# A column of zeros, written by GpSimd behind every single gather of the three edge passes

## The reference

```python
x = _layernorm(x + _L0_gnn_ref(x, edge_index, ...))            # max over edges of relu([x_i, x_j - x_i] @ W1 + b1) @ W2 + b2
x = _layernorm(x + _L1_gnn_ref(x, edge_index, edge_attr, ...)) # mean of edge_attr by src, then a two-layer network
x = _layernorm(x + _L2_gnn_ref(x, src, dst, ...))              # mean over edges of x[src], gates, linear
x = _layernorm(x + _L3_gnn_ref(x, ntype, etype, src, dst, ...))# attention of 4 heads over edges, typed weights
```

## Time and profile before

| | us |
|---|---|
| time, median of 2 runs | 19,879.55 (19,871.68 to 19,887.42) |
| the profiled execution: span from first to last instruction | 21,982.3 |
| busy in it: POOL, DVE, PE, PEld, ACT | 15,097.0, 6911.8, 4774.0, 4149.9, 1772.2 |
| gathers, 3 x 3125, busy in b, c, d | 3014.6, 3299.2, 3021.6 |
| scatter-adds, 3125, busy | 4984.9 |

### The profile page before, as it was taken

The page is one execution under the profiler, slowest core; times in us unless marked ns, Lnnn a source line. Parts: engine busy times, 40 slices in busy tenths (PEclk is TensorE's granted clock), DMA queues, the critical chain, the costliest instruction groups (busy, mean ns, idle before and its releaser), DMA issues. The chain is left out here.

```text
span 21982.3 us, 148548 instructions
## 1 busy us (share of the span) xinstructions
PE 4774.0 (22%) x30182; PEld 4149.9 (19%) x30182; DVE 6911.8 (31%) x16401; ACT 1772.2 (8%) x6281; POOL 15097.0 (69%) x13304
## 2 busy tenths in 40 slices
PE   4444444444423333333320000000041000000002
PEld 4444444444412222222210000000031000000001
DVE  3333333333312222222241111111122444444444
ACT  1111111111100000000010000000021000000001
POOL 5888888888876666666657777777724666666664
PEclk8555555555555555555555555555576555555555
DMA  4444444444422222222231111111122222222222
GB/s 93 53 52 52 52 52 53 50 53 52 52 48 65 65 65 65 63 65 64 65 59 48 47 47 46 47 47 46 43 68 89 87 89 89 87 90 87 89 89 38
DMA packets 1456154, 1380.95 MB, mean 63 GB/s; under 512 B 777810, under 2 KB 1260924, under 8 KB 1455996
## 3 DMA queue, kind: packets, MB, share of 16 engines
q0 software_dynamic: 775408, 541.25, 17.1%
q1 hardware_dynamic: 662716, 736.98, 10.3%
q10 hardware_dynamic: 18000, 102.41, 1.1%
HBM read 762.18 MB, written 617.56 MB: 63 GB/s over the span
## 5 line engine op out<-in xcount | busy, mean ns | idle before, releaser
L500 POOL DMA_INDIRECT agg<-sums,ag_idx x3125 | 4984.9, 1595 | 1166.4 <-issue 1118.5
L534 POOL DMA_INDIRECT gat<-tab_t,gi x3125 | 3021.6, 967 | 1752.5 <-issue 928.0
L534 POOL DMA_INDIRECT gat<-tab_b,gi x3125 | 3014.6, 965 | 1752.6 <-issue 931.3
L534 POOL DMA_INDIRECT gat<-tab_x,gi x3125 | 3299.2, 1056 | 1100.9 <-issue 1061.1
L842 PE MATMUL bank<-at,same 128*128 128x64 f32 x6250 | 1882.7, 431 | 3281.7 <-issue 1057.3
L842 PEld LDWEIGHTS bank<-at,same 128*128 128x128 f32 x6250 | 1570.5, 311 | 3419.7 <-issue 1813.5
L908 PE MATMUL pair<-ident,tails 128*64 128x128 f32 (+1 forms) x20 | 4.9, 419 | 9304.2 <-DVE tails L1209 4931.4
L908 PEld LDWEIGHTS pair<-ident,tails 128*64 128x64 f32 (+1 forms) x20 | 3.0, 167 | 9305.2 <-DVE tails L1209 4931.6
L1302 DVE TENSOR_TENSOR run_sb<-p,gat 128x320 f32<-128x320 f32 x625 | 317.1, 507 | 3710.6 <-DMA gat<-tab_x,gi 3710.6
L1164 DVE TENSOR_TENSOR run_sb<-p,bank 128x320 f32<-128x320 f32 x625 | 304.9, 488 | 3177.7 <-remote 2346.6
L876 PE MATMUL bank<-ident,ub 128*128 128x128 f32 x1250 | 413.0, 434 | 3494.1 <-DVE ub L1192 2228.1
(11 more groups left out here) (263 smaller groups left out, 13806.5 us busy)
## 6 DMA issues: line engine op xcount, KB each, us to landing
edge<-start_rows SPq DMA_DIRECT2D x250, 800.0 KB
run<-run_sb SPq DMA_DIRECT2D x250, 800.0 KB
run<-run_sb SPq DMA_DIRECT2D x125, 900.0 KB
start_rows<-zeros ACTq DMA_DIRECT2D x125, 800.0 KB, 3.5
at<-in_edge_attr SPq DMA_DIRECT2D x125, 800.0 KB
tab_t<-trow SPq DMA_DIRECT2D x98, 512.0 KB, 2.6
agg<-sums,ag_idx POOLq DMA_INDIRECT x3125
gat<-tab_b,gi POOLq DMA_INDIRECT x3125
```

The costliest lines, as they stand in the source:

```text
L500: pool.indirect_dma_start(agg_d[r], rows(agg_d[r], ag_idx[:, k, r:r + 1]), sums[:, k, r, :], None, bounds_check=AGR - 1, oob_is_err=True, ...
L534: pool.indirect_dma_start(gat[:, k, s, 0:width], None, table, rows(table, gi[tp][:, s, k:k + 1])).then_inc(g_in[c][k], 16)
```

## The change

In each of the three passes a function `breathe` is called behind every gather. It waits until the memset behind the gather before has completed (`p_beat` has reached the number of memsets so far), has a no-op that carries this wait, and lets GpSimd write zeros into a new column `beat` of 128 x 1 numbers; this counts `p_beat` up by one. The first memset of all has no wait. `done` carries the count over from pass to pass. Nothing reads `beat`.

```diff
--- before.py
+++ after.py
@@ -127,6 +127,7 @@
         iota_bf = sb("iota_bf", [P, P], BF16)
         spare_i = sb("spare_i", [P, 1], I32)
         spare = sb("spare", [P, 1])
+        beat = sb("beat", [P, 1])
         marks = sb("marks", [P, 20])
         eps_c = sb("eps_c", [P, 1])
         far_c = sb("far_c", [P, 1])
@@ -285,6 +286,7 @@
         ch_pre, ch_k = sem("ch_pre"), sem("ch_k")
         ch_n = {c: sem(f"ch_n{c}") for c in "123"}
         o_out = sem("out_written")
+        p_beat = sem("pool_beat")
 
         def run_view(tp, width):
             return run_sb[tp][:, :, 0:KS * width].rearrange("p s (k f) -> p s k f", f=width)
@@ -522,6 +524,13 @@
             for i in range(2):
                 pool.wait_ge(l_out[i], 16 + 8 * NBAT)
 
+            def breathe(c, n, opening):
+                done = "bcd".index(c) * NG * SUB
+                if done or not opening:
+                    pool.wait_ge(p_beat, n + done)
+                    pool.nop(nofuse=True)
+                pool.memset(beat[:], 0.0).then_inc(p_beat, 1)
+
             def gathers(c, table, width, staged, per, used):
                 def body(t, tp, first):
                     pool.wait_ge(staged, (t + 1) * per)
@@ -533,6 +542,7 @@
                         for s in range(SUB):
                             pool.indirect_dma_start(gat[:, k, s, 0:width], None, table,
                                                     rows(table, gi[tp][:, s, k:k + 1])).then_inc(g_in[c][k], 16)
+                            breathe(c, t * COLS + (k * SUB + s), first and k + s == 0)
                 each_iteration(pool, body)
 
             def node_rows(c, run_d, car, width, n):
```

## The result

| | before | changed | ratio |
|---|---|---|---|
| median, us (2 runs each) | 19,879.55 | 20,049.8 (20,048.06 to 20,051.54) | 1.0086 [1.0069, 1.0103] |
| profiled execution: span, us | 21,982.3 | 20,046.3 | |

The change costs 170 us, 0.9%, where 1169 us were forecast. The profiled execution of the changed kernel is no longer than its runs, so profiling by itself does not lengthen this kernel. There is no trace of the kernel before at 19,880 us. Every ratio of an experiment is against the kernel before on its own chip.

What follows compares the result with a forecast made beforehand. GpSimd's gathers, 1.25 us each, were taken to bound the three edge passes. Memset 844, wait 46 and fetches 279 us sum to 1169 us on 19,879.55, giving 21,049 us (chance 0.53), range 19,850 to 22,280 us.

Steps and rivals of the forecast that it cites:

- The bound: Three edge passes: GpSimd's row of gathers, 1.25 us each, sets the time; what is added to the pitch adds 9375 times.
- The premise on the 2103 us: Profiled execution is 2103 us longer than the median; runs without a profile were taken to have hardly any of the stalls.
- The memset, 844 us: Behind each gather on GpSimd: one memset adds 0.09 us, 9375 times, 844 us; bounds 0.03 and 0.12 us each.
- Rival 4: Between gathers: the 0.30 us gap vanishes behind a memset, 0.20 us gained per gather, -1875 us, 18,005 us; chance 0.08.
- The estimate from its cycles, 390 us: Memset part priced by the skill page: 50 cycles at 1.2 GHz, 0.042 us a memset, 390 us in place of 844.
- The wait, 46 us: GpSimd's sequencer: new wait hidden behind the current gather, except 0.25 us at 186 back edges: 46 us, bounds 0 and 75.
- The fetches, 279 us: Loop bodies grow, so an instruction fetch pause shows 1.5 us per round trip, 186 times: 279 us, bounds 0 and 446.
- Rival 1: Edge passes: a memset costs 0.03 us and fetches nothing, 281 us, 20,161 us; chance 0.17.
- Rival 2: Stalls of b and d exist without a profile and absorb the memsets; only pass c pays, 374 us, 20,254 us; chance 0.10.
- Rival 3: Each memset is paid like a gather with its own gap, 0.40 us, 3750 us in all, 23,630 us; chance 0.12.
- a distance of under 1.29 us: Sign that the forecast is wrong: two gathers' starts under 1.29 us apart in the changed profile, where 1.34 was expected.

Runs made afterwards that it cites:

- f2: Changed kernel with two one-column memsets behind each gather, the second one counting: 21,606.66 us, 0.9826 of the kernel before.
- e3: Changed kernel with a memset of 128x128 instead of 128x1: 21,776.28 us, 0.9853 of the kernel before.
- e4: Changed kernel with a memset of 128x512 instead of 128x1: 23,956.89 us, 1.0902 of the kernel before.
- f1: Changed kernel with a 128x512 memset, each waiting for the memset two back, so one more gather is queued: 23,801.37 us, 1.0823 of the kernel before.
- e5: Changed kernel with two more sequencer no-ops behind each memset: 21,818.82 us, 0.9873 of the kernel before.
- e6_waits_only: Changed kernel without memset: register operation, always fulfilled wait and two no-ops behind each gather, the second counting: 21,550.56 us, 0.98 of the kernel before.

## Why the prediction was wrong

**The bound** was right: the passes go at GpSimd's pitch, 1.25 us, and what lengthens the distance between gathers lengthens the time. The premise on the 2103 us was half right. The first runs seem indeed to have hardly any of the stalls: take the changed kernel's time outside its three passes, 20,046 - 12,054 = 7992 us, off the 19,880 us, and 11,888 us are left for the passes, by this estimate 170 us over the bare pitch. The reason given, that the stalls come of profiling, was wrong: the changed kernel's profiled execution has hardly any (12 us), and on other chips the runs of the kernel before take 22,000 us too.

**The memset, 844 us: this is the step that failed.** The prediction put it as "Bounds: 0.03 and 0.12 us; below, nothing, if it fits into the 0.30 us between two gathers. I take 0.09 us, because a one-column instruction behind a long one of another kind is the nearest case". The end that it named and didn't take is what happened: the cost is 0, for one and for two memsets (f2), whose gathers start 1.249 us apart like those before. The rows of the start give what a memset costs in a queue of memsets, but the pitch of the gathers is not the sum of what is queued. It has 0.30 us in which the engine can do something else, of which 0.16 remained behind the memset in e3, e4 and f2. The mistake was to let these two alternatives, a free slot and a serial price, share one term: a cost of zero should have been a rival with a chance of its own. Rival 4 had the other half of it: the gap is used, but doesn't vanish behind a memset.

The Trainium skill, "GPSIMD Engine Reference", section 2.1, says that the completion of one instruction doesn't hold back the next; the two memsets 0.03 us apart in f2 agree. The estimate from its cycles, 390 us, added to the time what runs in a gap: measured was 0.

**The wait, 46 us.** The run-ahead of one gather is enough in the usual stretch, as predicted: the median distance did not change. At the back edges no distance stands out either, their median is 1.249 us in pass b as well; 0 us, the lower bound.

**The fetches, 279 us.** Right in kind and wrong in cause: a pause that the longer queue hides comes bare when one gather is queued, f1 against e4 shows it. The price of one was nearly right: 2.3 us, less 0.6 covered, is 1.68 us, where the prediction had 2.4 less 0.9, 1.5 us. But it comes 99 times, every 95 gathers, and not 186 times, once per round trip: 167 us. That this is near 279 us is partly luck, since the pauses of the loops are not those of the earlier trace rows: they come without instruction packets, and e5 excludes the number of instructions.

The Trainium skill, "Runtime: NRT & Kernel Launch", section Instruction fetch mechanics, has the crossing of a block mostly hidden. In the gather loops here the regular pauses hang neither on the number of instructions nor on packets of the instruction queues, so nothing in these runs contradicts it.

**The rivals.** Rival 1 came nearest in time (20,161 us), with a mechanism that isn't this one: the cost was in pauses and not in memsets. Rival 2, that the stalls of b and d stay and cover the change, did not hold in the changed kernel's first profile, which has none; where such stalls are, on the other chips, the change even gains. Rival 3 is refuted by the pitch.

**What would show it**: the text named the test that it then failed, a distance of under 1.29 us, and the trace has 1.25.

**A better version** than before on these chips is e6_waits_only, with 2% less; it has no memset. Whether it gains, costs or does nothing where the kernel before takes 19,880 us was not measured, since no experiment ran on such a chip.

## What to carry to other kernels

Where a queue of equal DMA instructions has a constant gap in front of each, price a small instruction between them both ways, in the gap and in series, and give each its chance. The wait that shortened the queue cost nothing at the median here; it cost at the rare long pauses that the queue used to hide. So look for them in the sequencer's records, compare the same places in both traces, and find by another count what they are tied to. Whether they are fetches, the packets of the instruction queues say. And compare the span of the profile with the runs: where they differ by 10%, the profile may show another regime, in which the same edit has another sign.

## What the runs showed of the hardware

- Behind a gather of 0.94 us GpSimd is free for 0.30 us; one or two memsets of 128x1 fit there at no cost, 128x128 lengthens the distance of two gathers by 0.085 us, 128x512 by 0.41 us.
- GpSimd's sequencer pauses for 2.3 us (2.87 us between two records in place of 0.55) once every 95 gathers of 128 rows. With gathers 1.25 us apart 1.68 us of it show with one gather queued, 0.43 us with two, nothing with five; with gathers 1.65 us apart two hide it.
- On the four chips of the experiments many sequencer records of SyncE, and in some kernels of GpSimd, last 0.70 us in place of 0.02 to 0.05 while gathers start 1.25 us apart, and the kernel before takes 22,000 us there, 19,880 where it was first timed. The cause is open.
